# Float16 projections, a reordered attention, and one image's statistics gathered inside the other's attention

## What is computed

```python
# layer 0
x = x + _L0_conv_ref(_gn(x), W_qkv, W_out, rel_height, rel_width)
# layer 1
x = x + _L1_conv_ref(_gn(x), weight, bias)
```

## Time and profile before

| | |
|---|---|
| median of 3 runs | 4075.92 us (4075.8 to 4081.03) |
| the profiled execution's own time | 4075.55 us |
| its span, first to last instruction | 4073.7 us |
| PE busy | 3749.2 us, 92% |
| DVE busy | 3363.8 us, 83% |
| ACT busy | 2831.7 us, 70% |
| POOL busy | 2108.6 us, 52% |
| TensorE's mean granted clock | 0.992 of full speed |
| DMA | 462.47 MB, mean 114 GB/s |

### The profile page before, as it was taken

How to read it: one execution, slowest core, us unless ns; L and a number is a source line. 1 busy time by engine, 2 the same in 40 slices (tenths; PEclk the granted TensorE clock), 3 DMA queues, 4 the chain that set the end, 5 groups by cost and what they waited for, 6 DMA issues and landing times. The chain is left out here.

```text
span 4073.7 us, 129480 instructions
## 1 busy us (share of the span) xinstructions
PE 3749.2 (92%) x48644; PEld 2632.9 (65%) x48644; DVE 3363.8 (83%) x5614; ACT 2831.7 (70%) x4805; POOL 2108.6 (52%) x2823
## 2 busy tenths in 40 slices
PE   0099999999999999999999999999958999999999
PEld 0077777777777777777777777777743444444444
...
GB/s 400 293 67 93 91 77 93 90 78 93 88 80 93 85 83 93 83 84 93 82 86 93 81 87 93 77 90 93 68 69 162 152 149 153 151 154 151 154 145 93
DMA packets 490076, 462.47 MB, mean 114 GB/s; under 512 B 9408, under 2 KB 469056, under 8 KB 469184
## 3 DMA queue, kind: packets, MB, share of 16 engines
...
## 5 line engine op out<-in xcount | busy, mean ns | idle before, releaser
L631 POOL TENSOR_TENSOR sb_erel<-sb_brel 128x288 f32<-128x288 f32 x512 | 351.0, 686 | 1018.6 <-DVE sb_brel L502 1018.4
L896 POOL TENSOR_TENSOR sb_tf<-sb_cf 128x1024 f32<-128x1024 f32 x256 | 609.3, 2381 | 393.7 <-DVE sb_tl L878 371.4
L401 PE MATMUL ps_t<-sb_ident,sb_d 128*108 128x128 f32 x4096 | 662.5, 284 | 1.7 <-ACT sb_pt L595 1.7
L421 PEld LDWEIGHTS ps_s<-sb_kf,sb_qb 128*64 128x64 f32 x16384 | 519.7, 138 | 182.2 <-issue 177.3
L535 DVE TENSOR_TENSOR sb_qb<-ps_q,sb_own_head 128x1024 f32<-128x1024 f32 x512 | 621.6, 1214 | 15.6 <-PE ps_q L386 15.6
L804 PE MATMUL ps_c<-sb_th,sb_wc_h 128*128 128x512 f16 x1536 | 584.9, 381 | 40.4 <-DVE sb_tl L878 40.4
L434 PEld LDWEIGHTS ps_v<-sb_wq,sb_zf 128*108 128x108 f32 x4096 | 511.3, 173 | 153.8 <-issue 81.4
L647 POOL TENSOR_TENSOR sb_prod<-sb_rel,sb_shift 128x192 f32<-128x192 f32 x1024 | 502.8, 512 | 198.7 <-DVE sb_rel L511 198.7
L421 PE MATMUL ps_s<-sb_kf,sb_qb 128*64 128x54 f32 x16384 | 586.1, 225 | 9.7 <-issue 6.5
L804 PE MATMUL ps_c<-sb_th,sb_wc_l 128*128 128x512 f16 x1536 | 583.9, 380 | 0.0
L804 PE MATMUL ps_c<-sb_tl,sb_wc_h 128*128 128x512 f16 x1536 | 583.8, 380 | 0.0
...
## 6 DMA issues: line engine op xcount, KB each, us to landing
sb_xb<-rows SPq DMA_DIRECT2D x128, 780.0 KB, 6.0
...
sb_abuf<-rows SPq DMA_DIRECT2D x32, 2048.0 KB, 11.7
sb_x<-rows SPq DMA_DIRECT2D x128, 512.0 KB, 3.8
x<-sb_x SPq DMA_DIRECT2D x128, 512.0 KB, 4.1
...
```

The costliest lines, as they stand in the source:

```text
L401: last = pe.transpose(ps_t[0:KV, wj * 128:(wj + 1) * 128], d[:, at:at + KV], ident[:])
L421: last = pe.matmul(s_at, qb[:, qc:qc + QB], kf[:, kc:kc + KR], start=True, stop=True)
L631: pool.tensor_tensor(view(erel, 0, 128, 0, [[KN, PAIRS], [KS, KS], [1, KS]]), view(brel, 0, 128, 0, [[KS, PAIRS], [0, KS], [1, KS]]), view ...
L896: pool.tensor_tensor(tf[:, k * TF:(k + 1) * TF], view(cf, 0, 128, c0 + ra * W, [[2 * W, PAIRROWS], [1, W]]), view(cf, 0, 128, c0 + rb * W, ...
```

## The change

1. wq becomes wq_h and wq_l in float16, and z gets float16 parts zh and zl beside a float32 zf of two slots in place of four. Each of q, k and v is the sum of three float16 products (PRODUCTS) in place of one float32 matmul. ScalarE casts zh (high), GpSimd subtracts zl, one plane a group each.
2. The output projection gets a bank of its own, ps_y; the output keeps one bank, ps_o, in place of two. VectorE's x1 update moves behind the reciprocal, bn_stats of x1 ahead of q's eviction, tmax into group 1 and tmin into group 2. ScalarE's Exp of group n-1 comes at the end of group n, in place of Exp of n-2 at its beginning; zf is made in groups 2 and 3 of one unit and 0 of the next.
3. The prologue gathers only the first image's statistics (A_TILES = 256 / 16). The convolution's weights are formed on GpSimd.
4. In units 6 to 37 SyncE loads 8 rows of the second image into st, 1 MB a unit, and VectorE takes four bn_stats of them in groups 0, 2 and 3. In unit 38 the second image's moments and tables are made: bn_aggr in group 0, the group sums in group 1 (TensorE's matmul writes ps_q ahead of q), the tables in group 2. Units 38 to 41 are written out between two loops.

The new functions moments_sums, moments_group and moments_tables hold the operations of L129 to L166 for a list of images. The core of the diff:

```diff
-        wq = sb("wq", 3 * C, F32)
+        wq_h, wq_l = sb("wq_h", 3 * C, F16), sb("wq_l", 3 * C, F16)
         wo = sb("wo", C, F32)
         wc_h, wc_l = sb("wc_h", TAPS * C, F16), sb("wc_l", TAPS * C, F16)
...
         tmin = sb("tmin", UNITS * 4, F32)
 
-        def groupnorm_moments(phase):
+        def moments_sums(dve, link, batches, agg_done):
+
+            half = UNITS * 6
+            for b in batches:
+                link(dve.bn_aggr(aggr[:, 2 * b:2 * b + 2], stats[:, b * half:(b + 1) * half]))
+            b0, bn = batches[0], len(batches)
+            mean = view(aggr, 0, 128, 2 * b0, [[2, bn]])
+            var = view(aggr, 0, 128, 2 * b0 + 1, [[2, bn]])
...
+
+            dve.tensor_tensor(var, var, gn[0][:, b0:b0 + bn], ALU.add).then_inc(agg_done, 1)
+
+        def moments_group(dve, link, batches, ps, sum_done):
+
+            b0, bn = batches[0], len(batches)
...
+        def moments_tables(dve, link, batches, sqrt_done):
+
...
-        A_TILES = ROWS // A_ROWS
+        A_TILES = H // A_ROWS
...
                     dve.tensor_scalar(wneg[:], wscale[:, 2:3], -1.0, None, ALU.mult)
...
-                    dve.tensor_copy(wc_h[:], gw[:, 0:TAPS * C]).then_inc(w_hi, 1)
                     dve.tensor_copy(wo[:], rawn[:, SPANS[1][0]:SPANS[1][1]])
-                    dve.tensor_copy(wq[:], rawn[:, 0:3 * C])
+                    dve.tensor_copy(wq_h[:], rawn[:, 0:3 * C]).then_inc(w_qh, 1)
+                    dve.wait_ge(w_qh, 1)
+                    dve.tensor_tensor(wq_l[:], rawn[:, 0:3 * C], wq_h[:], ALU.subtract)
...
-                    dve.wait_ge(w_hi, 1)
-                    dve.tensor_tensor(wc_l[:], gw[:, 0:TAPS * C], wc_h[:], ALU.subtract)
...
-            groupnorm_moments("gn0")
+                    pool.wait_ge(w_norm, 1)
...
+                    pool.tensor_copy(gm[0], kw[0])
...
+                    pool.wait_ge(w_norm, 4)
+                    pool.tensor_copy(wc_h[:], gw[:, 0:TAPS * C]).then_inc(w_hi, 1)
+                    pool.wait_ge(w_hi, 1)
+                    pool.tensor_tensor(wc_l[:], gw[:, 0:TAPS * C], wc_h[:], ALU.subtract)
+            groupnorm_moments("gn0", (0,))
...
-            zf = sb("zf", 4 * PAR * PLANE, F32, pb)
+            zf = sb("zf", 2 * PAR * PLANE, F32, pb)
+            zh, zl = sb("zh", 4 * PAR * PLANE, F16, pb), sb("zl", 4 * PAR * PLANE, F16, pb)
...
-            ps_o = ps("ps_o", 1024)
+            ps_o, ps_y = ps("ps_o"), ps("ps_y")
...
-            TURNS = (UNITS - 3 - FIRST) // LOOP
+            STRIPS_1 = STRIPS // B
+            EARLY = STRIPS_1 // LOOP
+            GN = FIRST + LOOP * EARLY
+            SECOND = GN + LOOP
+            LATE = (UNITS - 3 - SECOND) // LOOP
...
+            GROUP_STEPS = 2 + 5
...
                 for u in range(-3, FIRST):
...
+                    body(u, u // 2, u % 4, some, None, False)
+                for first, turns, stat in ((FIRST, EARLY, True), (SECOND, LATE, False)):
+                    with eng.bass.Fori(0, turns, engines=[eng.engine], hint_back_edge=True) as i:
+                        for c in range(LOOP):
+                            body(i * LOOP + (first + c), i * (LOOP // 2) + (first + c) // 2, (first + c) % 4, every,
+                                 (i * LOOP + c, i * (LOOP // 2) + c // 2) if stat else None, False)
+                    if stat:
+                        for u in range(GN, SECOND):
+                            body(u, u // 2, u % 4, some, None, u == GN)
...
+            PRODUCTS = ((zh, wq_h), (zh, wq_l), (zl, wq_h))
...
-                def body(u, s, slot, on):
+                def body(u, s, slot, on, stat, moments_due):
...
+                    if stat is not None:
+
+                        row = settled(sp, (stat[0] + STRIPS_1) * WS + PAD)
+                        sp.wait_ge(sem["st_used"], (stat[0] + 1) * PAR)
+                        sp.dma_start(st[:, h * STW:(h + 1) * STW],
+                                     x_in[:, bass.ds(row, WS), :].rearrange("p a b -> p (a b)")
+                                     ).then_inc(st_loaded[h], 16)
...
-                    need(pe, sem["x1_done"], n - 2 * GROUPS)
+                    pe.wait_ge(sem["zl_done"], piece + 1)
                     need(pe, sem["qb_done"], piece)
-                    pe.matmul(ps_q[:, 0:QP], wq[:, 0:C], z_at(slot, p, KS + 1, [[KS, UW // 2], [1, QS]]),
-                              start=True, stop=True).then_inc(sem["q_mm"], 1)
+                    if moments_due:
+                        pe.wait_ge(sem["gn_agg_done"], 1)
+                        pe.matmul(ps_q[:, 0:2], gsum[:], aggr[:, 2:4], start=True, stop=True
+                                  ).then_inc(sem["gn_sum_done"], 1)
+                        pe.wait_ge(sem["gn_step_done"], GROUP_STEPS)
+                    for c, (z, w) in enumerate(PRODUCTS):
+                        last = pe.matmul(ps_q[:, 0:QP], w[:, 0:C], z_at(z, slot, p, KS + 1, [[KS, UW // 2], [1, QS]]),
+                                         start=(c == 0), stop=(c == 2))
+                    last.then_inc(sem["q_mm"], 1)
...
-                    pe.matmul(ps_k[:, 0:PLANE], wq[:, C:2 * C], z_at(slot, p, 0, [[1, PLANE]]),
-                              start=True, stop=True).then_inc(sem["k_mm"], 1)
+                    for c, (z, w) in enumerate(PRODUCTS):
+                        last = pe.matmul(ps_k[:, 0:PLANE], w[:, C:2 * C], z_at(z, slot, p, 0, [[1, PLANE]]),
+                                         start=(c == 0), stop=(c == 2))
+                    last.then_inc(sem["k_mm"], 1)
...
-                                last = pe.matmul(ps_v[0:KV, p * C:(p + 1) * C],
-                                                 z_at(vslot, p, GW * WK * vg, [[1, KV]]),
-                                                 wq[:, 2 * C:3 * C], start=True, stop=True)
+                                for c, (z, w) in enumerate(PRODUCTS):
+                                    last = pe.matmul(ps_v[0:KV, p * C:(p + 1) * C],
+                                                     z_at(z, vslot, p, GW * WK * vg, [[1, KV]]),
+                                                     w[:, 2 * C:3 * C], start=(c == 0), stop=(c == 2))
...
-                            need(pe, sem["of_done"], m - 1)
+                            need(pe, sem["of_done"], m)
...
-                            need(pe, sem["qb_done"], QB_BEFORE(n))
                             need(pe, sem["x1_done"], n - 2 * GROUPS)
                             ob = slot % 2
-                            pe.matmul(ps_q[:, 0:QP], wo[:], of[:, ob * 1024 + g * QP:ob * 1024 + (g + 1) * QP],
+                            pe.matmul(ps_y[:, 0:QP], wo[:], of[:, ob * 1024 + g * QP:ob * 1024 + (g + 1) * QP],
...
+                        dve.wait_ge(st_loaded[h], stat[1] * 16 + 16)
+                    for c in range(first, first + count):
+                        dve.bn_stats(stats[:, bass.ds(stat[0] * (PAR * 6) + (UNITS * 6 + c * 6), 6)],
+                                     st[:, h * STW + c * 512:h * STW + (c + 1) * 512]
+                                     ).then_inc(sem["st_used"], 1)
...
-                        if on(u - 2 if g else u - 3, UNITS):
...
-                                                     oscale[:, 0:1], view(x1, 0, 128, off, dims), ALU.mult, ALU.add
-                                                     ).then_inc(sem["x1_done"], 1)
...
+                        if on(u - 2 if g else u - 3, UNITS):
...
+                                                     view(ps_y, 0, 128, 0, [[1, QS], [QS, UW // 2]]),
+                                                     oscale[:, 0:1], view(x1, 0, 128, off, dims), ALU.mult, ALU.add
+                                                     ).then_inc(sem["x1_done"], 1)
+                        if moments_due and g == 1:
+                            moments_group(dve, link, (1,), ps_q, sem["gn_sum_done"])
...
+                        if g == 0 and on(u - 3, UNITS):
+
+                            dve.wait_ge(sem["x1_done"], (u - 2) * PAR)
+                            for c in range(2):
+                                dve.bn_stats(stats[:, bass.ds((u - 3) * 12 + c * 6, 6)],
+                                             x1[:, (1 - h) * WS * UW + c * 512:(1 - h) * WS * UW + (c + 1) * 512])
...
-                        if g == 0 and on(u - 3, UNITS):
...
-                        if g == 2 and on(u - 3, UNITS):
...
-                            last.then_inc(sem["x1_read"], 16)
+                        if g in (1, 2) and on(u - 3, UNITS):
+
+                            t, op = ((tmax, ALU.max), (tmin, ALU.min))[g - 1]
+                            dve.tensor_reduce(t[:, bass.ds((u - 3) * 4, 4)],
+                                              view(x1, 0, 128, (1 - h) * WS * UW, [[TILE, 4], [UW, WS], [1, TILE]]),
+                                              AX.XY, op).then_inc(sem["x1_read"], 8)
+                        if stat is not None:
+                            if g != 1:
```

(48 more changed lines are left out.)

222 lines of the change are left out of this document (108 added, 114 removed).

## The result

The changed kernel takes 3846.35 us (3843.86 to 3849.51), the kernel before 4076.81 (4075.8 to 4081.03) beside it: a ratio of 0.943 [0.942, 0.945]. The forecast was 3706, its range 3650 to 3830. The direction was right, the gain of 370 was 230, and the time lies 16 us above the range.

What follows compares the result with a forecast made beforehand. TensorE was taken to bound the attention and VectorE the prologue. From 4075.55 us, -294.8 for the attention, -81.5 for the prologue and +7 for the moments gave 3706, range 3650 to 3830.

Steps and rivals of the forecast that it cites:

- So TensorE bounds a plain unit; I add 0.2 us for such collisions and take 19.2: Attention units without statistics: four TensorE groups make 19.0 us, plus 0.2 for collisions, 19.2 (18.6 to 19.7).
- Rival 1: Projection v: float16 weight loads bind at 90 ns each, a group of 5.16 us, total 3882; chance 0.11.
- rival 2's half case: Attention: VectorE waits 0.82 us for ScalarE's late Exp in half of the groups, total 3799; whole rival's chance 0.16.
- the sum of 3706: Whole kernel: 4075.55 less 294.8 for the attention, less 81.5 for the prologue, plus 7 for the moments.
- upper end of 3775: Whole kernel: high end of the forecast's own range, from units of 19.6 and 20.9 with the other terms' high ends.
- Prologue, -81.5: Prologue: 128 bn_stats fewer (-76.0), convolution weights to GpSimd (-4.4), one bn_aggr and table copies fewer, first projection later (+3).
- attention starts near 102: End of the prologue: a sign of the forecast being right, the attention starting near 102 us.
- Float16, a group of 4.75: TensorE's projections q, k, v as three float16 products each: save 0.47 us, a group of 4.75 in place of 5.22.
- "just in time" walk of Exp: Reordered attention: Exp ends about 5.4 us after TensorE's scores, ssum wants it at 5.5; 0.3 to 0.4 later behind zf.
- Statistics' units, 20.3: 32 attention units with four more bn_stats: VectorE bounds them at 20.3 us a unit (19.9 to 21.3).
- rival 3: Statistics' load lands 1 to 3 us late in each of 32 units: +32 to +96, total 3738 to 3802; chance 0.08.
- Moments, +7: Second image's moments inside the attention: 8.0 us of linked VectorE work, slack takes about one, +7 (3 to 12).

Runs made afterwards that it cites:

- after: The changed kernel as first written, without padding, against the kernel before: 3846.35 us, ratio 0.943.
- exp_head: Against pad243: ScalarE's Exp of the group before moved to the head of its next group; 3774.97 us, ratio 0.926 to the kernel before.
- pad243: Against the changed kernel: 243 more instructions (waits already met) in TensorE's idle prologue, moving both attention loops' places; 3720.14 us, ratio 0.913 to the kernel before.
- st_first: Against pad243: SyncE issues the load of st ahead of x and xb; 3713.08 us, ratio 0.910 to the kernel before.
- placed kernel: Same as pad243: the changed kernel with 243 more instructions in TensorE's prologue; 3720.14 us.

## Why the prediction was wrong in its size, and where it was right

**The step that failed** is "So TensorE bounds a plain unit; I add 0.2 us for such collisions and take 19.2". The plain unit is 20.91. Of the excess of 1.71, 1.60 is TensorE waiting for its own program at the jump and running at the lower clock behind it, and 0.11 what the terms of the sum had wrong. These 0.11 are small by luck: two errors, +0.31 for the group and -0.20 for collisions that did not come, nearly cancel. I treated TensorE's time as the sum of its matmuls; the change gave it a second loop and four units written out between them, and moved where the late loop's end falls. The kernel before showed a jump of 0.357 us in each turn; I had not looked at it, and by itself it would not have told that this cost hangs on the place. None of the four rivals held it. Rival 1's 3882 and rival 2's half case of 3799 lie around the result, but their signs (v starts 90 ns apart; ssum over 100 us in 1000) are absent from after: 55 ns and 69.7. With the loop placed, the sum of 3706 meets 3720.14, 14 us off. The range's lack was the case "something outside the engines". (The sum's own upper end of 3775 adds up to 3772.)

**Prologue, -81.5.** The first scores moved from 208.64 to 122.59, -86.0. The last bn_stats end at 93.0, where I had 92.4, and the one bn_aggr takes 3.62, for 3.64 in the sum (timeline of after, merged):

```profile
79.85 13.13 DVE L286 BATCH_NORM_STATS2 sb_stats<-sb_abuf 128x512 f32 x22
...
93.31 3.62 DVE L118 BATCH_NORM_AGGREGATE sb_aggr<-sb_stats 128x2 f32<-128x768 f32 x1 [0.32 <-PEq L225]
```

The moments' tables are done at 102.4, as forecast, yet "attention starts near 102" was loosely put: the first q waits for the load, zf, cast and subtraction until 113.2. The gain beyond the sum, 4.5 us, lies in this stretch: q comes 82.6 earlier than before (195.82), and the four projections from the first q to the first scores take 9.4 us, not 12.8.

**Float16, a group of 4.75.** Measured 4.83. k is 0.50 (starts 1700.17 to 1700.67) and v with its gap 0.77 (to 1701.44), as forecast; q is 0.41, not 0.33: 137 ns for a pass of 256 columns, where k's 396 take 167. k and the convolution stream at 0.42 ns a column, q at 0.53. q reads z in runs of 4 columns, k the plane in one piece; that this is the reason is argued only. Twelve v matmuls start 55 ns apart, so rival 1 is out. The load under them, and the cast and the subtraction on ScalarE and GpSimd (ns: least, median, greatest):

```profile
L496 PEld LDWEIGHTS ps_v<-sb_wq_h,sb_zh x2048: 127/128/216, 133.9 to 2772.6; 128*108 128x108 f16 x187
```

```profile
L714 ACT CAST sb_zh<-sb_zf x512: 503/522/559, 111.6 to 2731.4; 128x396 f16<-128x396 f32 x171
```

```profile
L761 POOL TENSOR_TENSOR sb_zl<-sb_zf,sb_zh x512: 932/940/956, 112.2 to 2734.7; 128x396 f16<-128x396 f32 x171
```

The load is recorded with 128 ns, between the 98 and 132 of the earlier trace rows, where I had put it, and the loads follow each other every 55 ns with their matmuls. The 90 ns that the rule of the Trainium skill, "TensorE: Matmul & The Clock Gate", *LDWEIGHTS (loading the stationary operand)*, gives for 108 columns as an estimate do not bind here. Cast and subtraction are 0.52 and 0.94 for 0.5 and 0.92.

**The reordered attention, +0.2 for collisions.** The price was 0 in float32 (20.88 = 4 x 5.22) and 0 in float16 (19.31 = 4 x 4.83). The "just in time" walk of Exp was right by a small margin, as exp_head shows.

**Statistics' units, 20.3.** Measured 20.55 to 20.60. In pad243 VectorE is busy 384 of 400 us there and waits 13.6 for st, 0.7 a unit; so rival 3 was true in kind, and small, for st_first without that wait takes off only 0.08. The price of bn_stats was right: each is recorded with 0.683 us, but the next instruction starts 0.59 to 0.61 after it, as in the prologue (recorded 0.675, 0.594 apart). What makes up the rest of the excess is not shown. Whole run of pad243:

```profile
L548 DVE BATCH_NORM_STATS2 sb_stats<-sb_st x128: 672/683/696, 238.8 to 891.8; 128x512 f32 x128
```

**Moments, +7.** Unit 38 takes 29.47 against 19.31: +10.2, within 3 to 12. Its two gaps in TensorE's timeline after are the links that I named; q waits behind them:

```profile
902.66 0.56 PE L440 MATMUL ps_q<-sb_aggr,sb_gsum 128*128 128x2 f32 x2 [1.00 <-DVE sb_aggr L124]
...
905.34 0.40 PE L444 MATMUL ps_q<-sb_zh,sb_wq_h 128*128 128x256 f16 x1 [2.11 <-DVE sb_gn L137]
```

A wait of 2.2 us for "issue" at 895 is in this unit as well; a packet of its program lands at 896.1, and TensorE goes on at 897.5.

**Balance** of the spans, placed kernel against before (4073.7 to 3718.7, -355.0): start -85.8, attention from the first to the last scores -267.2 (2782.2 to 2515.0), the rest -2.0. The stalls then give back 123.3 (3842.0 - 3718.7), all of it in the attention. The sum had -81.5 and -287.8 in the first two; the 20.6 that are missing are 0.11 x 96, 0.25 x 32 and 3.2 of the moments, 22, less what the last units make good.
